# Attention sums kept in SBUF, result rows loaded at once over two queues at the end, expert weights sent by SP from a row number in a register

## The reference

```
xn = layernorm(x)
out = x + attention(xn) + experts(xn)

attention: q, k, v = silu(causal_conv4(xn @ W)); beta = sigmoid(xn @ W_b)
           delta rule over chunks of 32 steps, 4 heads of 32:
             per chunk: invert a 32x32 triangular system, then u = T v, w = T k
             recurrence over chunks: u' = u - w S; o = q S + local u'; S = S + k^T u'
           short (3) and long (31) causal filters of v
           gates = softmax(gelu([xn, fir_s, fir_l, delta] @ W_fuse1) @ W_fuse2)
           o = gated sum of fir_s, fir_l, delta, v; rmsnorm; @ W_o
experts:   top 2 of 8 experts for each of 4096 tokens, softmax weights
           y_e = (g sigmoid(g) l) @ W3,  g, l = z @ Wg, z @ Wl,  z = (xn@W1)(xn@W2)
```

## Time and profile before

| | value |
|---|---|
| median of 3 runs (lowest, highest) | 904.22 us (900.74, 907.99) |
| profiled execution | 901.63 us, of which span 899.9 us |
| busy share PE / DVE / POOL / ACT | 74% / 62% / 56% / 33% |
| mean granted TensorE clock | 0.812 |
| transfers | 69.10 MB, 77 GB/s over the span |

### The profile page before, as it was taken

One profiled execution on the slowest core, in us unless ns is written; L12 is line 12 of the kernel. 1 busy time (PEld: TensorE's weight loads), 2 busy tenths in 40 slices (PEclk: granted clock), 3 DMA queues, 4 the chain that ended last, 5 costly groups with the idle time before them and its releaser, 6 DMA issues.

```text
span 899.9 us, 30793 instructions
## 1 busy us (share of the span) xinstructions
PE 662.3 (74%) x13276; PEld 506.4 (56%) x13276; DVE 556.5 (62%) x1233; ACT 298.8 (33%) x519; POOL 508.1 (56%) x565
## 2 busy tenths in 40 slices
PE   3345749788877896887796797778787887896741
PEld 2235737566656665665664565566565666674531
DVE  6899875548447747576538545774467665723651
ACT  2210043424335235243343343332434352313120
POOL 3722178848682864768724847756857654521311
PEclk9555569989789798888997898988969996878585
DMA  8212123232122131132221321422323302113341
GB/s 314 111 59 70 60 54 76 71 99 54 63 76 71 49 90 62 41 89 80 75 55 40 89 47 53 112 84 39 68 74 85 96 8 56 52 22 103 113 140 70
DMA packets 62950, 69.10 MB, mean 77 GB/s; under 512 B 40080, under 2 KB 45200, under 8 KB 62688
## 3 DMA queue, kind: packets, MB, share of 16 engines
q0 software_dynamic: 10672, 34.78, 13.6%
q1 hardware_dynamic: 51712, 30.42, 11.8%
q10 hardware_dynamic: 432, 1.94, 0.5%
HBM read 47.45 MB, written 19.66 MB: 75 GB/s over the span
## 4 chain that ended last, share of the span: by engine, by line
PE 27%; POOL 26%; issue 18%; DVE 17%; DMA 6%; ACT 4%; SPq 2%; POOLq 0%; DVEq 0%; ACTq 0%
POOL y_d L1034 6%; POOL xs L1009 4%; PE ps_shared L1614 4%; PE ps_g L1610 4%; POOL z L1068 3%; PE ps_x L1610 3%; DVE acc L1380 3%; POOL ssq_o L1060 3%; PE ps_shared L1752 2%; PE ps_l L1610 2%; PE ps_shared L1610 2%; DMA w_mid<-y_d 2%; POOL sumsq L974 2%; PE ps_shared L1619 1%; PE ps_shared L1668 1%
## 5 line engine op out<-in xcount | busy, mean ns | idle before, releaser
L1034 POOL DMA_INDIRECT y_d<-work,put_i x92 | 92.4, 1004 | 45.2 <-issue 26.5
L1009 POOL DMA_INDIRECT xs<-xn_d,owner_i x92 | 94.2, 1024 | 28.2 <-issue 26.3
L1610 PE MATMUL ps_g<-z,w_mid 128*128 128x512 f32 x276 | 87.7, 461 | 27.3 <-POOL z L1068 23.4
L1610 PE MATMUL ps_x<-xr,w_up 128*128 128x512 f32 x276 | 97.2, 468 | 12.3 <-issue 10.8
L1610 PEld LDWEIGHTS ps_g<-z,w_mid 128*128 128x128 f32 x276 | 58.1, 220 | 45.8 <-issue 33.4
L1380 DVE SCALAR_TENSOR_TENSOR acc<-pre,late_sb,acc 128x512 f32<-128x512 f32 x72 | 59.6, 828 | 39.0 <-ACT acc L1127 38.1
L1068 POOL TENSOR_TENSOR z<-work,z 128x512 fp32r<-128x512 f32 x46 | 59.8, 1299 | 39.1 <-ACT z L1234 38.7
L1610 PE MATMUL ps_l<-z,w_mid 128*128 128x512 f32 x276 | 79.1, 423 | 0.0
L1581 DVE SCALAR_TENSOR_TENSOR work<-ps_g,w_plain,work 128x512 f32<-128x512 f32 x46 | 34.3, 746 | 54.1 <-ACT work L1240 54.0
L1610 PEld LDWEIGHTS ps_x<-xr,w_up 128*128 128x128 f32 x276 | 53.7, 218 | 24.1 <-issue 11.5
L1240 ACT ACTIVATE work<-ps_g,w_plain 128x512 f32<-128x512 f32 x46 | 31.5, 685 | 103.0 <-PE ps_g L1610 103.0
(11 more groups left out here) (248 smaller groups left out, 1493.8 us busy)
## 6 DMA issues: line engine op xcount, KB each, us to landing
xa_d<-xr SPq DMA_DIRECT2D x8, 512.0 KB, 2.7
xa<-xa_d SPq DMA_DIRECT2D x8, 512.0 KB, 3.7
w_mid<-y_d SPq DMA_DIRECT2D x16, 256.0 KB, 3.4
system_d<-masked SPq DMA_DIRECT2D x8, 256.0 KB
x_res<-hidden SPq DMA_DIRECT2D x8, 256.0 KB, 2.8
part_d<-x_res SPq DMA_DIRECT2D x8, 256.0 KB
comb<-part_d SPq DMA_DIRECT2D x8, 256.0 KB, 2.8
out<-comb SPq DMA_DIRECT2D x8, 256.0 KB, 2.0
```

The lines of the kernel that those rows point to most:

```text
L1009: pool.indirect_dma_start(xs[par][:, c, :], None, xn_d.rearrange("w p (c d) -> (w p c) d", c=CPW), bass.IndirectOffsetOnAxis(owner_i[:, w ...
L1034: pool.indirect_dma_start(y_d, bass.IndirectOffsetOnAxis(put_i[:, w * CPW + c:w * CPW + c + 1], 0), y_sb[par][:, c * D:(c + 1) * D], None) ...
L1610: made = pe.matmul(to, weights[a], x[b], start=start and n == 0, stop=stop and n == 2)
```

## The change

- The attention sums of `store` are written to 8 places in SBUF (`total`): 4 tiles `comb`, the dead `qkv_raw` part of `early_sb`, and three pieces of `taps`, which are dead once the last long filter is done (`TAPS_LATE`, windows 5 to 7, whose `store` waits for it). The write to `part_d` and the load back are gone; `x_res` of the next window waits for the sum alone.
- `fetch` no longer belongs to a ring: every window has its own dead buffer (two in `w_up`, two in `w_mid`, four pairs of `z` parts). SP loads the first expert row of every window and ACT the second, 8 transfers each, after the last scatter has landed. `combine` adds into `total[w]`; `give` stores it.
- `load_split` and `load_plain` move from POOL to SP, as plain transfers whose row number is read from `row_i` into a register.
- `FLOW` names the new engines, `PULL` has other numbers and `LEAN` is filled, so all five lists are written in another order. One line of each table is shown below.

```diff
-    "load_split": [[(POOL_, 1.2, 7.0)]], "load_plain": [[(POOL_, 1.2, 5.0)]], "split_up": ...
+    "load_split": [[(SP_, 1.2, 6.0)]], "load_plain": [[(SP_, 1.2, 4.0)]], "split_up": ...
-    "fetch": [[(SP_, 1.8, 4.5)]], "combine": [[(DVE_, 3.0)], [(SP_, 0.5, 2.5)]],
+    "fetch": [[(SP_, 0.7, 5.0), (ACT_, 0.7, 5.0)]], "combine": [[(DVE_, 3.2)]], "give": [[(SP_, 0.5, 2.5)]],
-PULL = {"beta_T": -100, "blend": 100, "choose": -200, "combine": -400, "conv": -150, "conv0": 150, "count": 300,
+PULL = {"beta_T": -200, "blend": -600, "choose": 400, "combine": -250, "conv0": 50, "count": -200, "delta_T": 50,
-LEAN = {}
+LEAN = {"beta": -30, "beta_T": 45, "blend": 45, "combine": -15, "conv": -30, "delta_again": -40, "fetch": -10,
+TAPS_LATE = range(5, WINDOWS)
...
         yield "out", w, 0, bk
+        if w >= WINDOWS - len(TAPS_LATE):
+            yield need(("fir_l", PAIRS - 1, PARTS - 1))
         yield "store", w, 0, bk
...
+    def fetch(w):
+        yield need(("y_put", TILES - 1, 0), ("y_put", TILES - 2, 0))
+        yield "fetch", w, 0, None
     def combine(w):
-        yield need(("store", w, 0), ("y_put", TILES - 1, 0), ("y_put", TILES - 2, 0))
-        if w >= 2:
-            yield need(("combine", w - 2, 0))
-        yield "fetch", w, 0, None
+        yield need(("store", w, 0), ("fetch", w, 0))
         yield "combine", w, 0, None
...
+        total = [tile[:].rearrange("p c d -> p (c d)") for tile in comb] + [qkv_raw] + [
+            taps_flat[:, n * TILE:(n + 1) * TILE] for n in range(len(TAPS_LATE))]
+        y12 = [[tile[:, k * TILE:(k + 1) * TILE].bitcast(FP) for k in range(2)] for tile in (w_up[0], w_up[1], w_mid, w_mid[:, GLW:])]
+        y12 += [[z[e][j][part][:, :].bitcast(FP) for part in range(2)] for e in range(2) for j in range(FJ)]
...
+                elif name == "load_split":
+                    sp.wait_ge(S["placed"], 1)
+                    if w:
+                        sp.wait_ge(S["up_low"], w)
+                        sp.wait_ge(S["mid_low"], w)
+                    row = sp.value_load(row_i[0:1, w:w + 1], min_val=0, max_val=(EXPERTS - 1) * P)
+                    sp.dma_start(w_split[:, :], expert_split[bass.ds(row, P), :]).then_inc(S["in_split"], 16)
...
                 elif name == "fetch":
-                    sp.wait_ge(S["in_part"], 16 * (w + 1))
-                    if w < 2:
-                        for n in range(2):
-                            sp.wait_ge(S[f"in_y_d{n}"], 16 * CPW * ((TILES + 1 - n) // 2))
-                    else:
-                        sp.wait_ge(S["combined"], w - 1)
-                        sp.wait_ge(S["in_out"], 16 * (w - 1))
-                    sp.dma_start(flat(comb[par]), part_d[w]).then_inc(S[f"in_comb{par}"], 16)
-                    for k in range(2):
...
+                    for n in range(2):
+                        sp.wait_ge(S[f"in_y_d{n}"], 16 * CPW * ((TILES + 1 - n) // 2))
+                    sp.dma_start(y12[w][0], y_rows(0, w)).then_inc(S[f"in_y{w}"], 16)
...
-                    pool.indirect_dma_start(w_split[:, :], None, expert_split,
-                                            bass.IndirectOffsetOnAxis(row_i[:, w:w + 1], 0)).then_inc(S["in_split"], 16)
...
+                elif name == "fetch":
+                    for n in range(2):
+                        act.wait_ge(S[f"in_y_d{n}"], 16 * CPW * ((TILES + 1 - n) // 2))
+                    act.dma_start(y12[w][1], y_rows(1, w)).then_inc(S[f"in_y{w}"], 16)
...
-                    dve.tensor_tensor(flat, ps[:, :], flat, ALU.add).then_inc(S["summed"], 1)
+                    if w in TAPS_LATE:
+                        dve.wait_ge(S["fir_l_ps"], 2 * PAIRS)
+                    dve.tensor_tensor(total[w], ps[:, :], flat, ALU.add).then_inc(S["summed"], 1)
```

More of the change, by code:

```diff
@@ L109 @@
     "o_T": [[(PE_, 1.0)]], "o_T_out": [[(ACT_, 0.6)]],
[L110 removed]
+    "out": [[(PE_, 2.0)]], "store": [[(DVE_, 0.7)]],
 }
[L112 to L121 removed]
@@ new lines @@
+LEAN = {"beta": -30, "beta_T": 45, "blend": 45, "combine": -15, "conv": -30, "delta_again": -40, "fetch": -10,
+        "fir": -5, "fir_l_T": -25, "fir_s_T": 5, "full": 5, "fuse": -20, "fuse2": 40, "gate_T": 35, "gates": -30,
+        "give": 15, "inv": -35, "inverse_out": 10, "k_T": 25, "ln": -40, "load_x": -15, "load_xs": -5.2, "low": 30,
+        "mark": -30, "masks": -45, "mid_g": 12.1, "mid_l": -5.2, "mix_s": 10, "mix_v": 30, "norm": -35, "o_T_out": -25,
+        "owned": 10, "products": 45, "project": 5, "rank": 30, "rms": -5, "solve_in": -15, "split_mid": -3.5,
+        "state": 30, "store": 45, "sumsq": -15, "system": 25, "times": 10.4, "turn": -7.7, "u_adj": 25, "up2": -3.4,
+        "v_T": 40, "v_act": 30, "v_again": -40, "v_b": -60, "w_T": 15, "w_T_out": -30, "xn_out": -5, "y_out": -8.7,
+        "y_put": -10.4, "zlow": -15.6}
```

84 lines of the change are left out of this document (38 added, 46 removed).

## The result

| | before | after |
|---|---|---|
| median of 4 runs each (lowest, highest) | 905.58 us (900.74, 907.99) | 884.06 us (879.61, 884.19) |
| span of the profiled execution | 899.9 us | 882.4 us |
| mean granted TensorE clock | 0.812 | 0.842 |
| first and last `y_out` | 151.2, 809.4 | 156.5, 823.5 |
| transfers | 69.10 MB | 64.92 MB |

The changed kernel takes 0.9762 of the time before (95% interval 0.9731 to 0.9792), 21.5 us less between the medians and 17.5 us less between the two spans. The forecast was 872 us, in a range of 853 to 896. (The kernel before has one run more here than ahead of the prediction, so its median stands 1.4 us higher.)

A forecast was written before the change was run, and what follows sets the result against it. Two bounds were seen: a chain hopping between engines up to 809.4 us and a serial tail behind it. Terms -20 + 15.9 - 28.8 + 1 = -32 us from 904.2 gave 872 us, range 853 to 896.

The forecast's parts named there:

- step 1: Expert stage: POOL loses 46 weight transfers to SP; gain taken as 20 us, between nothing and 36.
- Step 3: Tail after the last `down`: recurrence follows at once, combines and HBM trip shortened; 61.7 us against 90.5, -28.8.
- step 2: Middle stage: PE work from behind the last `down` is done before it; cost taken as +15.9 us.
- step 4: Small ones: `x_res` waiting less, 0, and DVE list differences up to 112 us; +1 us, within -2 and +3.
- main case: Whole kernel: POOL relief 12 to 28 us, moved work 12 to 18, tail within 5; 860 to 884, chance 0.47.
- The bound of 36: Upper bound of the POOL relief: 23.6 us of transfer pieces with gaps plus 12.3 us of weight-transfer waits in the chain.
- A: Middle stage: PE takes up the slack, so freed POOL time gives nothing; 892 us, range 884 to 896, chance 0.24.
- B: Middle stage: POOL relief worth all its 36 us, moved PE work costs 8; 848 us, range 842 to 860, chance 0.16.
- C: SP's list: weight transfers caught behind attention waits, so slower; 938 us at 2 us per tile, over 913, chance 0.07.
- if it stands at 820 or later, A or C holds: Sign at the last `y_out`, forecast near 806 us; 820 or later would mean A or C.
- if the stage before it does not become shorter by its own 4 us: Sign before the tail: without a 4 us shortening despite added PE work, the forecast is wrong.
- PE's busy share there did rise over 81%: Sign for the moved work: PE's busy share between 150 us and the last `down` rises over 81%.

The follow-up runs named there:

- experiment 1: Kernel before with only the 46 weight transfers moved from POOL's list to SP's, other lists kept: 876.76 us, ratio 0.9711.
- experiment 2: Changed kernel with its 46 weight transfers put back on POOL, PE, DVE and ACT lists kept: 915.09 us, ratio 1.0109 to the kernel before.
- Experiment 5: Changed kernel with one product of the first expert stage done twice per tile, 69 matmuls added: ratio 0.9651 to the kernel before, second chip.
- experiment 6: Changed kernel with an unread POOL power ahead of each low part of z, 46 in all: ratio 0.9658 to the kernel before, second chip.
- experiment 9: Changed kernel beside the old lists with SP-issued weights and the new end, third chip: 963.70 us, 0.9646, and 955.63 us, 0.9552, to the kernel before.
- experiments 8: Kernel before, own lists, with weights issued by SP and the new end grafted on, fetches by SP alone: ratio 0.9536, second chip.
- experiment 7: Lists planned anew for the new end alone with old tables, then the 46 weight transfers moved from POOL to SP: ratio 0.9535 to the kernel before.
- experiment 3: Kernel before with only the new end, weights on POOL, old PULL and LEAN, lists planned anew: 899.3 us, ratio 0.9944.
- experiment 4: Changed kernel with the old PULL and empty LEAN, planned anew with the new FLOW: 890.74 us, ratio 0.9829 to the kernel before.
- experiment 10: Big weight transfer cut to 512 of 1536 words a row from the second tile: changed kernel 0.9610, old lists with both parts 0.9530, to kernel before.

## Why the prediction was right, and where its terms were not

The verdict (faster by over 1%) and the range were right, and so was the kind of mechanism in steps 1 and 3. The sum of -32 us was -17.5 between the spans, and step 2 was wrong in size and in reason. That the time still fell into the range is partly luck: step 1 and the tail gave 10 to 14 us more than reckoned, and steps 2 and 4 took 24 us more. At 884.06 us it lies just outside the main case (860 to 884). Term by term:

- **Step 1, the transfers leave POOL: forecast -20, measured -27 to -31.** The middle of experiment 1 is 26.8 us shorter, its median 27.5 us lower, and experiment 2 takes 31 back. The bound of 36 held. The failing phrase is the reason for taking only somewhat over half of it, "because PE has only 19% free in the stage". Experiment 5 shows that PE had room to spare at one place even in the changed kernel. The price per transfer was also read from the wrong side: I summed durations and gaps in the chain (23.6 us), and experiment 6 shows that durations alone are nearly free where POOL waits anyway. The 34.5 us of idle time ahead of the transfers in the rows were the better sign, though not a measure of the price (61.8 us in experiment 2, for about the same price). The wait for w_mid's split went from POOL's list as forecast; the one for `y_out` did not go but now stands ahead of the scatter (57.4 us). SP's side cost less than held: a register load took 0.27 us (the two lines of register loads above). The Trainium skill, "DMA: Bandwidth & Descriptors", section "Latency and other measured facts", gives a floor of about 600 ns; the measurement differs, and it decides. The masks and solved blocks were still waited for by SP, 89.6 and 78.5 us, against the 239.6 and 144.9 of the earlier trace rows.
- **Step 2, work moved ahead of the last `down`: forecast +15.9, measured +35.6**, as the difference between the middle of the changed kernel (667.0) and that of experiment 1 (631.4). On the third chip the same two orders differ by 25.6 us (experiment 9), so the size is 26 to 36 us. This is the term that failed, and in two places. The count was somewhat short: the 418 matmuls out of the tail are nearly the 426 that I took, but 255 more came from the stretch ahead of the first `y_out`. PE is busy 21.1 us longer in the middle (14.1 on the third chip) where 15.9 were forecast; at the density of experiment 1, 83%, 21.1 us cost 25.4. And the stage did not keep that density: 10.2 us more were lost (8.0 on the third chip). Part of this may lie on DVE. It is busy 17.7 us longer in the middle, while only 5.5 us left the tail. Over the whole span it needs 14.5 us more than in experiment 1 for the same 1233 instructions, because single ones take longer: the 8 of `k_n` (L1416, the normed keys of the attention) 10.6 us instead of 6.1, the 120 products of the triangular inverse 49.4 instead of 45.2. Experiment 5, where 19 us of added PE work at another place cost nothing that could be measured, suggests that PE's time is not the unit to price this in, and that what is paid is the chain of hand-overs between the engines that comes with real work. That reading was not isolated by a run.
- **Step 3, the tail: forecast 61.7, measured 58.9.** The last `u_adj` came 14.9 us behind the last `y_out`, not 16.5: the first rows had landed and were combined by 837.32, and PE delivered at about 838.3, behind a pause of 2.57 us. A pause of 2.43 us stood at this place before, too, in the timeline of the kernel before:

```profile
846.80 0.43 PE L1614 MATMUL ps_shared<-state,kq_T 32*32 32x32 f32 x14 [2.43 <-issue]
```

  From the last `u_adj` to the end of the changed kernel's span it was 44.0 us against the 45.2 reckoned. The combine between mixes, the one ahead of the gates and the trip through HBM went as forecast. But the saving was largely not a net one: 418 of 984 matmuls left the tail for the middle. Where the order was kept (experiments 8 and 9) the tail stayed long (88.5 us) and the kernel was still the faster; where 935 matmuls left it (experiment 7) the kernel was no slower than that.
- **Step 4: forecast +1, measured +5.3**, of which 4.0 us are there when `row_i` is written (74.4 against 70.4). The bound was +3. No run took this stretch apart. The two other kernels of the first chip with lists planned anew have it too, with a first `y_out` at 158.6 (experiment 3) and 157.9 (experiment 4); where the lists stayed it stood at 150.8 (experiment 1). On the third chip it is only 0.9 us later in the new lists than in the old (159.7 against 158.8), so the size of this term is not settled.

**The rivals.** The time fell on the edge of A's range (884 to 896), and A was still wrong as a mechanism: it had PE take up POOL's slack, but step 1 gave 27 to 31 us, and added PE work cost nothing at the place where it was tried. A's own terms (step 1 at 0 to -8, step 2 at 19.6) add up to 888 to 896, so 884 was not in reach of them. Its range came near because step 2 and step 4 were 24 us dearer than reckoned and step 1 gave 7 to 11 more. B had step 1 about as near as I had (36, measured 27 to 31), and step 2 at half, where it was about twice. C did not happen. ACT's wait for `w_split` did grow, to 51.6 us, the sign that was named for it, but SP was ready for nearly every big transfer (the row under experiment 10), and 13 us less of that wait on the third chip gave 2 to 4 us.

**What would show it.** The mark "if it stands at 820 or later, A or C holds" was a bad one: the last `y_out` stood at 823.5 and neither held, because it mixes step 1 with step 2. The mark "if the stage before it does not become shorter by its own 4 us" told the failure, and rightly: by it the forecast was wrong on the middle stage. PE's busy share there did rise over 81%, to 81.8%, which shows how little that sign was worth.

**Left open.** Why the new lists make the middle 35.6 us longer than the old ones with the same issuer: neither PE's load, nor POOL's, nor the time that the weights take to land was shown to be the cause. DVE's longer instructions, the late release of w_split's buffer and the planning with POOL relieved (experiment 7) are untested. Also open is why the changed kernel loses 78 us of span on the third chip (960.0 against 882.4) where PE's busy time grows by 41. Which part of the 5 us of experiment 3 is the end itself also stays open, as does the split of the fetches over two queues, of which nothing was tried alone.

## What to carry to other kernels

On an engine that works through its list in order, do not price an instruction by its duration; look at the wait in front of it and at what stands behind it. Here 46 transfers on POOL cost 27 to 31 us, and 46 instructions of the same length, put where the engine waits anyway, cost 1, give or take 8. Work that is moved out of a serial tail into a busy stage is not hidden there because its engines are only 80% busy: the tail gave 26 to 32 us, and the stage took back 26 to 36. Count all of it on both sides of the cut, and compare the two orders before either is taken for the better. A part of a change can be worth as much alone as the whole, or more (0.9711 against 0.9762, and 0.9552 against 0.9646 with the old order kept). That is found only if it is run alone.

## What the runs showed of the hardware

- A register load from SBUF on SP takes 0.27 us, and 0.79 us pass from the end of SP's wait (91.57) to the start of the transfer (92.36). Pieces of the changed kernel's chain around the first weights (start, us, what):

```profile
91.57 0.03 SPq L850
...
91.64 0.27 SPq L851
...
91.95 0.15 SPq L851
...
92.36 4.18 DMA w_split<-expert_split
```

- The 786 KB of a `w_split` landed in 4.18 us when SP sent it as a plain transfer (the last of these lines); the two pieces of the earlier trace rows, sent by POOL, took 6.53 and 5.73 us. Other transfers may have been in flight there.
- 16 loads of 256 KB sent at once over two queues landed 3.5 to 9.8 us after their issue (medians of their groups), SP's 1.1 to 1.9 us sooner than ACT's in each pair. The DMA issues of the changed kernel (KB each, median us to landing):

```profile
z<-y_d SPq DMA_DIRECT2D x4, 256.0 KB, 8.3
z<-y_d ACTq DMA_DIRECT2D x4, 256.0 KB, 9.8
...
w_up<-y_d SPq DMA_DIRECT2D x2, 256.0 KB, 3.5
w_up<-y_d ACTq DMA_DIRECT2D x2, 256.0 KB, 4.6
```

- The same kernel takes 904 us on one chip and 999 to 1000 us on two others. In the changed kernel POOL, DVE and ACT are busy as long there as in the first profile, within 2% (456.9, 559.3 and 300.9 us against 458.6, 568.8 and 299.6). PE is busy longer, 699.1 against 658.0 us, at a mean granted clock of 0.808 against 0.842; its 276 matmuls into ps_x take 103.4 us, against 98.4.
